# Attention with a cumulative softmax: the half-column products of a unit together, the half-row products together, and the loop over pairs of heads written out

## The chip, the cores and the metric

One core of one Trainium2 chip. The metric is the device time of one execution in microseconds (us). All work lies on five engines: TensorE (PE in the rows; PEld is its loading of the stationary operand), VectorE (DVE), ScalarE (ACT), GpSimd (POOL) and SyncE (SP), which starts the transfers.

## The reference, cut to what matters

```python
x = x + 0.5 * ffn(layernorm(x))        # two experts, top 1
x = x + attn(layernorm(x))             # 16 heads, DK = M = 64, DV = 128, 2 x 1024 tokens
x = x + 0.5 * ffn(layernorm(x))
# attn, for each head, with s clipped to +-32
z = cumlogsumexp(s); g = exp(z_before - z); p = exp(s - z)
hk = hk * g + k (x) p;   ok = q . hk           # step by step over the tokens
pv = softmax(ok)
hv = hv * g + p (x) v;   ov = pv . hv
o = rmsnorm(ov) * silu(gate) @ Wo
```

## The kernel before, in words

The two feed-forward phases are not touched. The attention (`phase_attention`) runs over 8 pairs of heads and, in each pair, over 4 units of 512 tokens (`UNIT`, 4 chunks of 128): 32 units. The first unit of each sequence (`first`) starts from an empty state. The pairs 0 to 6 are the body of a hardware loop on every engine (`Fori`), the last pair is written out, because it also normalises and routes the rows for the last phase.

Inside a unit k of a pair i the recurrence is done in chunks: with e = exp(s) and its running sum z, `ok` is masked scores times e plus the query times the state `hk`, all divided by z; `pv` is its softmax; `ov` is masked scores of pv and e times v, plus pv times the state `hv`. All products that TensorE makes for it stand in the program of one unit in a fixed order, and beside them the projections of the next unit (`project_q`, `project_k`, `project_s`, four `project_vg`: each 12 products of 128x512, in the lines `turned` L1197 and L1223) as filling while other engines work. The order on TensorE before:

1. `project_q(k+1)`; the chunk states `dk` = kn . en (L1284); the scores q . k (L1291); `project_k(k+1)`
2. masked scores times e (L1301); query times `hk` (L1305); `project_s(k+1)`; `okT` turned (L1311); `project_vg` 0; `pv` turned (L1319); `project_vg` 1
3. scores of pv and e, "b" (L1327); the chunk states `dv` = en . v (L1334); masked b times v (L1342); pv times `hv` (L1347); `project_vg` 2 and 3
4. the normed output `u` turned (L1364); e and k of the next unit turned (`turn_ek`, L1260 and L1264); the output projection of this unit, 24 products (L1377)

Two heads are worked on together, 64 rows of the array each. So there are three kinds of product: those over the whole array; those in half columns (the output is 64 partitions high: dk, masked scores times e, dv), written 128\*64 in the rows of the profile; and those in half rows (64 values are summed: scores, b, pv times `hv`), written 64\*128. A product of float32 operands stands in the trace as two; so a run of 8 in the program is x16 there. The projections use fp32r operands split in a high and a low part and stand there once.

VectorE does in a unit: the reciprocal of z (L1072), the running sums of `hk` (L1081, L1083), the mask on the scores (L1088), the copy of k (`k_copy`, L987), `okT` (L1096), the softmax (L1101 to L1109), the mask on b (L1120), the running sums of `hv` (L1128, L1130), gates (L1007), the sum z of the next unit (`z_scan`, L999), the sum of squares (L1152), `u` (L1159), the low part of u turned (L1170), the copy of k turned (`kn_copy`, L1012), and the additions of the output to `xres` (L1177). Its order is that of the program, and every operation waits on semaphores. Two banks of PSUM (`PJ`) take the projections in turn, so `project_q(k+1)` waits for the third gate of unit k, which frees the bank:

```python
def project_q(i, k):
    pe.wait_ge(gate_done, count(i, k, UC, -1))
    turned(i, k, 0, q_mm)
```

## Time and profile before

| | us |
|---|---|
| median of 3 runs | 2142.3 (2140.78 to 2146.86) |
| the profiled execution | 2142.46 |
| its span, first to last instruction | 2140.7 |
| TensorE busy in the span | 2012.2 (94%) |
| VectorE busy in the span | 1371.8 (64%) |
| ScalarE busy in the span | 666.3 (31%) |

The attention takes the span from about 467 to 1717 us. A busy share in the profile is the time in which an instruction of the engine is under way. TensorE's products overlap, so their starts tell more than their durations.

### The profile page before, as it was taken

The page shows a single profiled execution, that of the slowest core. Times are in us where ns is not written, and L with a number is a line of the kernel's source. Part 1 is how long each engine was busy: PE and PEld are TensorE (multiplying, and loading weights), DVE is VectorE, ACT ScalarE, POOL GpSimd, SP SyncE. Part 2 cuts the span into 40 slices and gives each one's busy share as a digit, 9 for nine tenths or more (in the row PEclk, how much of TensorE's full clock was granted, in tenths as well). Part 3 has the DMA queues.
Part 4 walks back from the last instruction along what each step waited for, and adds up shares of the span by engine and source line. Part 5 has one row for each costly group of instructions (what it writes and reads, how often), then busy time and mean ns, then how long its engine had stood idle before and what let it go on. Part 6 is the DMA issues. An engine that isn't in the chain of part 4 may idle for free. (4 is left out here: it accounts for less than half of the span.)

```text
span 2140.7 us, 30741 instructions
## 1 busy us (share of the span) xinstructions
PE 2012.2 (94%) x11848; PEld 1639.8 (77%) x11848; DVE 1371.8 (64%) x2702; ACT 666.3 (31%) x1207; POOL 276.2 (13%) x216
## 2 busy tenths in 40 slices
PE   2999999969999999999999999999999679999998
PEld 2788888847887878878878878878887558888786
DVE  5765667736666666666656666666667756665684
ACT  2443445523121121221212221221213134443452
POOL 2110111101020020120110110110201200110100
PEclk9999999989999999999999999999999789999999
DMA  6463436650010010000000100100100136433565
GB/s 216 142 184 128 134 115 190 202 173 8 1 38 9 1 38 9 17 29 1 28 19 1 38 9 1 38 9 1 38 1 20 40 134 211 128 103 115 149 191 182
DMA packets 54329, 165.14 MB, mean 77 GB/s; under 512 B 5424, under 2 KB 5424, under 8 KB 54192
## 3 DMA queue, kind: packets, MB, share of 16 engines
q1 hardware_dynamic: 46736, 145.80, 21.0%
q0 software_dynamic: 7456, 17.34, 3.9%
q8 instruction: 107, 1.75, 0.3%
q14 instruction: 30, 0.25, 0.0%
HBM read 137.40 MB, written 25.72 MB: 76 GB/s over the span
## 5 line engine op out<-in xcount | busy, mean ns | idle before, releaser
L1223 PE MATMUL at_pj<-at_w_lo,at_xT_hi 128*128 128x512 f32 x512 | 211.2, 413 | 0.0
L1223 PE MATMUL at_pj<-at_w_hi,at_xT_lo 128*128 128x512 f32 x512 | 202.5, 395 | 0.0
L1223 PE MATMUL at_pj<-at_w_hi,at_xT_hi 128*128 128x512 f32 x512 | 202.3, 395 | 0.0
L1197 PE MATMUL at_pj<-at_xT_hi,at_w_lo 128*128 128x512 f32 x384 | 159.2, 414 | 11.9 <-issue 11.1
L550 DVE TENSOR_TENSOR last_ff_w_lo<-last_ff_stage,last_ff_w_hi 128x1024 fp32r<-128x1024 f32 x80 | 98.0, 1225 | 89.3 <-ACT last_ff_w_hi L373 89.1
L1197 PE MATMUL at_pj<-at_xT_hi,at_w_hi 128*128 128x512 f32 x384 | 152.3, 397 | 0.0
L1197 PE MATMUL at_pj<-at_xT_lo,at_w_hi 128*128 128x512 f32 x384 | 151.9, 395 | 0.0
L550 DVE TENSOR_TENSOR first_ff_w_lo<-first_ff_stage,first_ff_w_hi 128x1024 fp32r<-128x1024 f32 x80 | 97.9, 1224 | 77.1 <-ACT first_ff_w_hi L373 76.9
L841 POOL TENSOR_TENSOR at_coef<-at_ms,minus_half 128x4 f32<-128x4 f32 x64 | 63.5, 1008 | 562.6 <-DVE at_ms L1155 562.6
L1177 DVE TENSOR_TENSOR xres<-at_r,xres 128x512 f32<-128x512 f32 x128 | 88.2, 689 | 66.7 <-PE at_r L1377 66.7
L826 POOL TENSOR_TENSOR at_w_lo<-at_stage,at_w_hi 128x1024 fp32r<-128x1024 f32 (+1 forms) x36 | 78.5, 2181 | 400.4 <-ACT at_w_hi L881 400.4
L935 ACT ACTIVATE at_pv<-at_ok 128x512 f32<-128x512 f32 x32 | 20.3, 634 | 333.6 <-DVE at_ok L1103 333.6
L373 ACT ACTIVATE last_ff_w_hi<-last_ff_stage 128x1024 fp32r<-128x1024 f32 x80 | 84.7, 1059 | 126.1 <-PE last_ff_ps_y L666 102.7
L373 ACT ACTIVATE first_ff_w_hi<-first_ff_stage 128x1024 fp32r<-128x1024 f32 x80 | 84.7, 1058 | 115.7 <-PE first_ff_ps_y L666 98.9
L652 PE MATMUL first_ff_ps_h<-first_ff_xT_hi,first_ff_w_lo 128*128 128x512 f32 (+1 forms) x320 | 113.0, 353 | 5.3 <-DVE first_ff_w_lo L550 3.3
L652 PE MATMUL last_ff_ps_h<-last_ff_xT_hi,last_ff_w_lo 128*128 128x512 f32 (+1 forms) x320 | 112.6, 352 | 4.5 <-DVE last_ff_w_lo L550 2.3
L1223 PEld LDWEIGHTS at_pj<-at_w_hi,at_xT_hi 128*128 128x128 f32 x512 | 96.3, 188 | 23.1
L1223 PEld LDWEIGHTS at_pj<-at_w_lo,at_xT_hi 128*128 128x128 f32 x512 | 96.4, 188 | 22.5
L652 PE MATMUL first_ff_ps_h<-first_ff_xT_lo,first_ff_w_hi 128*128 128x512 f32 (+1 forms) x320 | 112.1, 350 | 0.0
L652 PE MATMUL last_ff_ps_h<-last_ff_xT_lo,last_ff_w_hi 128*128 128x512 f32 (+1 forms) x320 | 111.9, 350 | 0.0
L652 PE MATMUL first_ff_ps_h<-first_ff_xT_hi,first_ff_w_hi 128*128 128x512 f32 (+1 forms) x320 | 111.9, 350 | 0.0
L652 PE MATMUL last_ff_ps_h<-last_ff_xT_hi,last_ff_w_hi 128*128 128x512 f32 (+1 forms) x320 | 111.7, 349 | 0.0
(315 smaller groups left out, 4785.6 us busy)
## 6 DMA issues: line engine op xcount, KB each, us to landing
first_ff_stage<-wff SPq DMA_DIRECT2D x90, 512.0 KB, 4.3
last_ff_stage<-wff SPq DMA_DIRECT2D x90, 512.0 KB, 4.2
at_stage<-watt SPq DMA_DIRECT2D x24, 512.0 KB, 3.5
at_stage<-watt SPq DMA_DIRECT2D x16, 384.0 KB, 3.2
xres<-x SPq DMA_DIRECT2D x4, 1024.0 KB, 9.9
mid_rows<-xres SPq DMA_DIRECT2D x4, 1024.0 KB, 7.6
out<-xres SPq DMA_DIRECT2D x4, 1024.0 KB, 7.8
first_ff_xg<-sorted_rows SPq DMA_DIRECT2D x3, 1028.0 KB, 5.3
```

Of the source, the lines that this page charges most:

```text
L373: act.activation(w_hi[:, t % RING, :], stage[:, t % RING, :], ACT.Copy).then_inc(w_hi_done, 1)
L550: dve.tensor_tensor(w_lo[:, t % RING, :], stage[:, t % RING, :], w_hi[:, t % RING, :].bitcast(F32), ALU.subtract).then_inc(w_lo_done, 1)
L652: last = pe.matmul(ps_h[t % 2][:, 0:width], w[:, r, k * P:(k + 1) * P], x[:, k, 0:width], start=(k == 0 and n == 0), stop=(k == KC - 1 and ...
L826: pool.tensor_tensor(w_lo[:, col:col + width], stage[:, 0:width], w_hi[:, col:col + width].bitcast(F32), ALU.subtract).then_inc(piece_lo, 1)
L841: pool.tensor_tensor(coef[:, cols], ms[:, cols], c["minus_half"][:, cols], ALU.pow).then_inc(coef_done, 1)
L935: act.activation(pv[:, :, :], ok[:, :, :], ACT.Exp).then_inc(pv_done, 1)
L1177: dve.tensor_tensor(xres[:, k * UC + cc, :], R[4 + cc % 2][:, :], xres[:, k * UC + cc, :], ALU.add).then_inc(added, 1)
L1197: last = pe.matmul(PJ[(7 * k + part) % 2][:, :], wq(w, kk, part), x[:, kk, tok], start=(kk == 0 and n == 0), stop=(kk == KC - 1 and n == 2))
L1223: last = pe.matmul(PJ[(7 * k + 3 + t) % 2][:, :], x[:, kk, tok], wvg(w, kk), start=(kk == 0 and n == 0), stop=(kk == KC - 1 and n == 2))
```

## The change

On TensorE the products of one kind stand together: dk, masked scores times e and dv (half columns) in one run; b, pv times `hv` and the scores of the next unit (half rows) in another. For that the scores of unit k+1 are made in unit k, with their mask, into a tile `am` that no longer serves b (b has `bm`); and the output projection of unit k moves into unit k+1, between `project_q` and `project_k`. The banks `R` are given out anew. VectorE makes the additions of a unit's output in the next unit, behind the reciprocal, copies k before the sums of `hk`, and makes the sums of `hv` ahead of the softmax. `okT` and `pv` give up their tiles. On all five engines the loop over pairs is written out. In the last pair the statistics of the rows are taken directly behind each addition.

```diff
+bm = sb("at_bm", [P, 2, UC, P])
...
 hv = sb("at_hv", [P, UC, DV])
-okT = sb("at_okT", [P, UNIT])
 ok = sb("at_ok", [P, UC, P])
-pv = sb("at_pv", [P, UC, P])
...
-        sp.dma_start(stage[:, 0:width], watt[bass.ds(pair, 1), :, col:col + width].rearrange("a p n -> (a p) n")).then_inc(piece_loaded, 16)
-    with sp.Fori(0, PAIRS - 1) as i:
+        sp.dma_start(stage[:, 0:width], watt[pair, :, col:col + width]).then_inc(piece_loaded, 16)
+    for i in range(PAIRS - 1):
...
-    with pool.Fori(0, PAIRS - 1) as i:
-        pair(i, False)
-    pair(PAIRS - 1, True)
+    for i in range(PAIRS):
+        pair(i, i == PAIRS - 1)
...
+        for cc in range(UC):
+            dve.wait_ge(wo_mm, count(i, k, UC, cc + 1))
+            dve.tensor_tensor(xres[:, k * UC + cc, :], R[2 + cc % 2][:, :], xres[:, k * UC + cc, :], ALU.add).then_inc(added, 1)
+            if with_statistics:
+                tile_statistics(i, k, cc)
+    def mask_a(i, k):
+        for b in range(2):
+            dve.wait_ge(a_mm, count(i, k, 2, b))
+            dve.tensor_tensor(am[:, b, :, :], R[2 + b][:, :].rearrange("p (a t) -> p a t", a=4),
+                              c["causal"][:, :].rearrange("p (a t) -> p a t", a=1).to_broadcast([P, 4, P]), ALU.mult).then_inc(a_masked, 1)
+    mask_a(0, 0)
     def pair(i, last_pair):
         for k in range(UNITS):
             more = not last_pair or k < UNITS - 1
             first = k % HALVES == 0
             dve.wait_ge(z_done, count(i, k, 1, 1))
             dve.reciprocal(rzT[:, :], zT[:, :]).then_inc(rz_done, 1)
+            if (i, k) != (0, 0):
+                add_out(*((i, k - 1) if k else (i - 1, UNITS - 1)), last_pair and k > 0)
+            if more:
+                k_copy(i, k + 1)
...
-            for b in range(2):
-                dve.wait_ge(a_mm, count(i, k, 2, b))
-                dve.tensor_tensor(am[:, b, :, :],
-                                  R[3 + b][:, :].rearrange("p (a t) -> p a t", a=4),
-                                  c["causal"][:, :].rearrange("p (a t) -> p a t", a=1).to_broadcast([P, 4, P]), ALU.mult).then_inc(a_masked, 1)
-            if more:
-                k_copy(i, k + 1)

             dve.wait_ge(ok_mm, count(i, k, 1, 0))
             dve.wait_ge(rz_done, count(i, k, 1, 1))
-            dve.tensor_tensor(okT[:, :], R[2][:, :], rzT[:, :], ALU.mult).then_inc(ok_scaled, 1)
...
-            dve.wait_ge(ok_tr, count(i, k, 1, 0))
...
-            if last_pair and k > 0:
-                for cc in range(UC):
-                    tile_statistics(i, k - 1, cc)
-                unit_statistics(k - 1)
-            for b in range(2):
-                dve.wait_ge(b_mm, count(i, k, 2, b))
...
+            dve.tensor_tensor(pT[:, :], R[2][:, :], rzT[:, :], ALU.mult).then_inc(ok_scaled, 1)
+
             dve.wait_ge(dv_mm, count(i, k, 1, 0))
             for cc in range(UC if first else UC - 1):
                 to = (cc + 1) % UC
...
+            dve.wait_ge(ok_tr, count(i, k, 1, 0))
...
+            if last_pair and k > 0:
+                unit_statistics(k - 1)
+            for b in range(2):
+                dve.wait_ge(b_mm, count(i, k, 2, b))
+                dve.tensor_tensor(bm[:, b, :, :],
...
+            if more:
+                mask_a(i, k + 1)
             if more:
                 gate_make(i, k + 1, 1)
                 z_scan(i, k + 1)
...
-            for cc in range(UC):
-                dve.wait_ge(wo_mm, count(i, k, UC, cc + 1))
-                dve.tensor_tensor(xres[:, k * UC + cc, :], R[4 + cc % 2][:, :], xres[:, k * UC + cc, :], ALU.add).then_inc(added, 1)
-                if not more:
-                    tile_statistics(i, k, cc)
             if not more:
+                add_out(i, k, True)
                 unit_statistics(k)
-    with dve.Fori(0, PAIRS - 1) as i:
-        pair(i, False)
-    pair(PAIRS - 1, True)
+    for i in range(PAIRS):
+        pair(i, i == PAIRS - 1)
...
+    def scores(i, k):
+        pe.wait_ge(q_out, count(i, k, 1, 1))
+        pe.wait_ge(k_out, count(i, k, 1, 1))
+        for cc in range(UC):
+            for h in range(2):
+                last = pe.matmul(R[2 + h][:, chunk(cc)], kT[half(h), chunk(cc)], qT[half(h), k % 2, chunk(cc)], start=True, stop=True)
+                if cc == UC - 1:
+                    last.then_inc(a_mm, 1)
+    def project_out(i, k, next_masked):
+        if k == 0:
+            pe.wait_ge(piece_lo, i * NP + 1 + 5)
+        if next_masked:
+            pe.wait_ge(a_masked, count(i, k + 1, 2, 2))
+        if i == PAIRS - 1 and k > 0:
+            pe.wait_ge(rows_ready, k)
+        for cc in range(UC):
+            if cc % 2 == 0:
+                pe.wait_ge(u_lo, count(i, k, 2, cc // 2 + 1))
+            if cc >= 2:
+                pe.wait_ge(added, count(i, k, UC, cc - 1))
+            for h in range(2):
+                for n, (x, w) in enumerate(((uT_lo, w_hi), (uT_hi, w_lo), (uT_hi, w_hi))):
+                    last = pe.matmul(R[2 + cc % 2][:, :], x[:, cc // 2, h, (cc % 2) * P:(cc % 2 + 1) * P], wo(w, h),
+                                     start=(h == 0 and n == 0), stop=(h == 1 and n == 2))
+            last.then_inc(wo_mm, 1)
     turn_ek(0, 0)
+    scores(0, 0)
...
             if more:
                 project_q(i, k + 1)
+            if (i, k) != (0, 0):
+                project_out(*((i, k - 1) if k else (i - 1, UNITS - 1)), True)
+            if more:
+                project_k(i, k + 1)

             pe.wait_ge(en_out, count(i, k, 1, 1))
             pe.wait_ge(kn_out, count(i, k, 1, 1))
-            pe.wait_ge(added, count(i, k, UC, 0))
             for cc in range(UC if first else UC - 1):
...
-            pe.wait_ge(q_out, count(i, k, 1, 1))
-            for cc in range(UC):
-                for h in range(2):
-                    last = pe.matmul(R[3 + h][:, chunk(cc)], kT[half(h), chunk(cc)], qT[half(h), b2, chunk(cc)], start=True, stop=True)
-                    if cc == UC - 1:
-                        last.then_inc(a_mm, 1)
-            if more:
-                project_k(i, k + 1)
-
-            pe.wait_ge(u_lo, count(i, k, 2, 0))
+            pe.wait_ge(added, count(i, k, UC, 0))
             pe.wait_ge(a_masked, count(i, k, 2, 2))
             for cc in range(UC):
                 for h in range(2):
                     last = pe.matmul(R[2][half(h), chunk(cc)], en[:, cc, half(h)], am[:, h, cc, :],
                                      start=(cc == 0), stop=(first and cc == 0), skip_group_check=True)
+            pe.wait_ge(v_out, count(i, k, UC, UC))
+            for cc in range(UC if first else UC - 1):
+                for h in range(2):
+                    last = pe.matmul(R[5][half(h), chunk(cc)], en[:, cc, half(h)], v[:, b2, cc, h * DV:(h + 1) * DV],
+                                     start=True, stop=True)
+            last.then_inc(dv_mm, 1)
             pe.wait_ge(hk_done, i * HK_AT[UNITS] + HK_AT[k + 1] + 1)
...
             pe.wait_ge(p_out, count(i, k, 1, 1))
+            pe.wait_ge(hv_done, i * HK_AT[UNITS] + HK_AT[k + 1] + 1)
             for cc in range(UC):
                 for h in range(2):
                     last = pe.matmul(R[4 + h][:, chunk(cc)], eT[half(h), b2, chunk(cc)], pT[half(h), chunk(cc)], start=True, stop=True)
                     if cc == UC - 1:
                         last.then_inc(b_mm, 1)
-            pe.wait_ge(v_out, count(i, k, UC, UC))
-            for cc in range(UC if first else UC - 1):
+            for cc in range(1 if first else 0, UC):
                 for h in range(2):
-                    last = pe.matmul(R[2][half(h), chunk(cc)], en[:, cc, half(h)], v[:, b2, cc, h * DV:(h + 1) * DV],
-                                     start=True, stop=True)
-            last.then_inc(dv_mm, 1)
+                    pe.matmul(R[h][:, chunk(cc)], pT[half(h), chunk(cc)], hv[half(h), cc, :],
+                              start=(cc == (1 if first else 0)), stop=False, skip_group_check=True)
+            if more:
+                scores(i, k + 1)
             for h in range(2):
                 pe.wait_ge(b_masked, count(i, k, 2, h + 1))
                 for cc in range(UC):
-                    last = pe.matmul(R[h][:, chunk(cc)], am[:, h, cc, :], v[:, b2, cc, h * DV:(h + 1) * DV],
-                                     start=(cc == 0), stop=(first and cc == 0), skip_group_check=True)
-            pe.wait_ge(hv_done, i * HK_AT[UNITS] + HK_AT[k + 1] + 1)
-            for cc in range(1 if first else 0, UC):
-                for h in range(2):
-                    last = pe.matmul(R[h][:, chunk(cc)], pT[half(h), chunk(cc)], hv[half(h), cc, :],
+                    last = pe.matmul(R[h][:, chunk(cc)], bm[:, h, cc, :], v[:, b2, cc, h * DV:(h + 1) * DV],
                                      start=False, stop=True, skip_group_check=True)
-                    if cc == UC - 1:
-                        last.then_inc(o_mm, 1)
+                last.then_inc(o_mm, 1)
             if more:
                 project_vg(i, k + 1, 2)
                 project_vg(i, k + 1, 3)
             if last_pair and k > 0:
                 pe.wait_ge(is1_done, k)
+                if more:
+                    pe.wait_ge(a_masked, count(i, k + 1, 2, 2))
                 pe.matmul(rt_later, c["later"][:], routing["is1"][:, tiles(k - 1)], start=True, stop=True).then_inc(rank_mm, 1)
                 pe.matmul(rt_total, c["ones"][:], routing["is1"][:, tiles(k - 1)], start=True, stop=True).then_inc(rank_mm, 1)
...
             if more:
                 turn_ek(i, k + 1)
-            if k == 0:
-                pe.wait_ge(piece_lo, i * NP + 1 + 5)
-            for cc in range(UC):
-                if cc % 2 == 0:
-                    pe.wait_ge(u_lo, count(i, k, 2, cc // 2 + 1))
-                if cc >= 2:
-                    pe.wait_ge(added, count(i, k, UC, cc - 1))
-                for h in range(2):
-                    for n, (x, w) in enumerate(((uT_lo, w_hi), (uT_hi, w_lo), (uT_hi, w_hi))):
-                        last = pe.matmul(R[4 + cc % 2][:, :], x[:, cc // 2, h, (cc % 2) * P:(cc % 2 + 1) * P], wo(w, h),
-                                         start=(h == 0 and n == 0), stop=(h == 1 and n == 2))
-                last.then_inc(wo_mm, 1)
-    with pe.Fori(0, PAIRS - 1) as i:
-        pair(i, False)
-    pair(PAIRS - 1, True)
```

In the order of the program on TensorE, the second unit, from the last product of a projection to the first of the next one, before (names: output <- moving, stationary operand; `x7` is seven more of the row):

```order
L1197 MATMUL at_pj<-at_xT_hi,at_w_hi 128x512
L1284 MATMUL at_r<-at_en,at_kn 64x64 [waits at_added,at_kn_out,at_en_out]
L1284 MATMUL at_r<-at_en,at_kn 64x64 x5
L1291 MATMUL at_r<-at_qT,at_kT 128x128 [waits at_q_out]
L1291 MATMUL at_r<-at_qT,at_kT 128x128 x7
L1206 REGISTER_ALU
L1197 MATMUL at_pj<-at_xT_hi,at_w_lo 128x512 [waits at_gate_done]
```

and with the change:

```order
L1201 MATMUL at_pj<-at_xT_hi,at_w_hi 128x512
L1319 MATMUL at_r<-at_en,at_kn 64x64 [waits at_kn_out,at_en_out]
L1319 MATMUL at_r<-at_en,at_kn 64x64 x5
L1326 MATMUL at_r<-at_am,at_en 64x128 [waits at_a_masked,at_added]
L1326 MATMUL at_r<-at_am,at_en 64x128 x7
L1331 MATMUL at_r<-at_v,at_en 64x128 [waits at_v_out]
L1331 MATMUL at_r<-at_v,at_en 64x128 x5
L1336 MATMUL at_r<-at_qT,at_hk 128x128 [waits at_hk_done]
L1336 MATMUL at_r<-at_qT,at_hk 128x128 x3
L1201 MATMUL at_pj<-at_xT_hi,at_w_lo 128x512 [waits at_q_out]
```

What moved: the scores have left, `project_k` no longer parts dk from the masked scores times e, and dv has come in from the later place.

Still TensorE, behind `project_vg` 1 in the same unit, before:

```order
L1223 MATMUL at_pj<-at_w_hi,at_xT_hi 128x512
L1327 MATMUL at_r<-at_pT,at_eT 128x128 [waits at_p_out]
L1327 MATMUL at_r<-at_pT,at_eT 128x128 x7
L1334 MATMUL at_r<-at_v,at_en 64x128 [waits at_v_out]
L1334 MATMUL at_r<-at_v,at_en 64x128 x5
L1340 REGISTER_ALU
L1342 MATMUL at_r<-at_v,at_am 128x128 [waits at_b_masked]
L1342 MATMUL at_r<-at_v,at_am 128x128 x3
L1342 MATMUL at_r<-at_v,at_am 128x128 [waits at_b_masked]
L1342 MATMUL at_r<-at_v,at_am 128x128 x3
L1347 MATMUL at_r<-at_hv,at_pT 128x128 [waits at_hv_done]
L1347 MATMUL at_r<-at_hv,at_pT 128x128 x7
```

and with the change:

```order
L1227 MATMUL at_pj<-at_w_hi,at_xT_hi 128x512
L1359 MATMUL at_r<-at_pT,at_eT 128x128 [waits at_hv_done,at_p_out]
L1359 MATMUL at_r<-at_pT,at_eT 128x128 x7
L1364 MATMUL at_r<-at_hv,at_pT 128x128 x8
L1276 MATMUL at_r<-at_qT,at_kT 128x128 [waits at_k_out,at_q_out]
L1276 MATMUL at_r<-at_qT,at_kT 128x128 x7
L1371 MATMUL at_r<-at_v,at_bm 128x128 [waits at_b_masked]
L1371 MATMUL at_r<-at_v,at_bm 128x128 x3
L1371 MATMUL at_r<-at_v,at_bm 128x128 [waits at_b_masked]
L1371 MATMUL at_r<-at_v,at_bm 128x128 x3
```

What moved: dv has left, pv times `hv` stands directly behind b, and the scores of the next unit follow.

Still TensorE, at the end of the same unit, from u to the first product of what follows, before:

```order
L1364 MATMUL at_r<-ident,at_u 128x128 [waits at_u_done]
L1364 MATMUL at_r<-ident,at_u 128x128 x3
L1364 MATMUL at_r<-ident,at_u 128x128 [waits at_u_done]
L1364 MATMUL at_r<-ident,at_u 128x128 x3
L1260 MATMUL at_r<-ident,at_eT 128x128 [waits at_e_done]
L1260 MATMUL at_r<-ident,at_eT 128x128 x3
L1264 MATMUL at_r<-ident,at_kT 128x128 [waits at_k_out]
L1264 MATMUL at_r<-ident,at_kT 128x128 x3
L1377 MATMUL at_r<-at_w_hi,at_uT_lo 128x512 [waits at_u_lo]
```

and with the change, where the projection of q follows directly:

```order
L1389 MATMUL at_r<-ident,at_u 128x128 [waits at_u_done]
L1389 MATMUL at_r<-ident,at_u 128x128 x3
L1389 MATMUL at_r<-ident,at_u 128x128 [waits at_u_done]
L1389 MATMUL at_r<-ident,at_u 128x128 x3
L1264 MATMUL at_r<-ident,at_eT 128x128 [waits at_e_done]
L1264 MATMUL at_r<-ident,at_eT 128x128 x3
L1268 MATMUL at_r<-ident,at_kT 128x128 [waits at_k_out]
L1268 MATMUL at_r<-ident,at_kT 128x128 x3
L1201 MATMUL at_pj<-at_xT_hi,at_w_lo 128x512 [waits at_gate_done]
```

What moved: the first product behind the turned k waits for a gate, where it waited for the low part of u.

## Rows read from the trace of the kernel before

**Rows 1.** The page of the profile: busy time, share of the span, instructions

```profile
PE 2012.2 (94%) x11848; PEld 1639.8 (77%) x11848; DVE 1371.8 (64%) x2702; ACT 666.3 (31%) x1207; POOL 276.2 (13%) x216
```

**Rows 2.** Stretches of the attention: us, busy per engine, then granted clock

```profile
650.00:800.00 150.00, 148.99 (x978) 121.13 (x979) 94.78 (x191) 32.62 (x69) 20.69 (x14) 0.99 0.06 17
1250.00:1400.00 150.00, 147.70 (x973) 119.78 (x972) 95.04 (x191) 32.61 (x69) 20.66 (x14) 0.99 0.06 17
1555.00:1595.00 40.00, 39.81 (x266) 32.22 (x267) 27.28 (x51) 8.12 (x18) 4.39 (x3) 1.00 0.00 1
```

**Rows 3.** TensorE in time order, first half of a unit: start, busy, group

```profile
842.23 0.39 PE L1197 MATMUL at_pj<-at_xT_hi,at_w_hi 128*128 128x512 f32 x1
842.55 0.57 PE L1284 MATMUL at_r<-at_en,at_kn 128*64 128x64 f32 x12
843.05 1.16 PE L1291 MATMUL at_r<-at_qT,at_kT 64*128 64x128 f32 x16
844.14 0.50 PE L1197 MATMUL at_pj<-at_xT_hi,at_w_lo 128*128 128x512 f32 x1
844.48 0.40 PE L1197 MATMUL at_pj<-at_xT_lo,at_w_hi 128*128 128x512 f32 x1
...
858.44 1.16 PE L1327 MATMUL at_r<-at_pT,at_eT 64*128 64x128 f32 x16
```

**Rows 4.** The same view, the end of the unit before

```profile
821.24 1.16 PE L1327 MATMUL at_r<-at_pT,at_eT 64*128 64x128 f32 x16
...
825.34 0.94 PE L1347 MATMUL at_r<-at_hv,at_pT 64*128 64x128 f32 x12
826.21 0.50 PE L1223 MATMUL at_pj<-at_w_lo,at_xT_hi 128*128 128x512 f32 x1
...
831.91 1.04 PE L1364 MATMUL at_r<-ident,at_u 128*128 128x128 f32 x8
...
834.01 0.47 PE L1377 MATMUL at_r<-at_w_hi,at_uT_lo 128*128 128x512 f32 x1 [0.19 <-DVE at_uT_lo L1170]
```

**Rows 5.** TensorE in time order, just behind an edge of the loop

```profile
650.51 0.50 PE L1197 MATMUL at_pj<-at_xT_hi,at_w_lo 128*128 128x512 f32 x1 [2.12 <-issue]
...
655.04 0.69 PE L1284 MATMUL at_r<-at_en,at_kn 128*64 128x64 f32 x16
655.66 1.16 PE L1291 MATMUL at_r<-at_qT,at_kT 64*128 64x128 f32 x16
```

**Rows 6.** The waits: engine and line, releaser, total us, times, longest

```profile
PEld at_pj L1197 <- issue: 13.7, 6, 2.6
```

**Rows 7.** VectorE in time order, the same unit

```profile
822.44 1.29 DVE L1120 TENSOR_TENSOR at_am<-at_r,causal 128x512 f32<-128x512 f32 x2 [2.78 <-PE at_r L1327]
...
825.02 0.42 DVE L1007 SCALAR_TENSOR_TENSOR at_gate<-at_gate,at_pj 128x256 f32<-128x256 f32 x1
...
827.01 0.69 DVE L1152 TENSOR_REDUCE at_ss<-at_u 128x4 f32<-128x512 f32 x1 [0.37 <-ACT at_u L954]
...
829.99 2.16 DVE L1159 SCALAR_TENSOR_TENSOR at_u<-at_r,at_coef,at_gate 128x128 f32<-128x128 f32 x8 [1.29 <-POOL at_coef L841]
833.17 0.69 DVE L1170 TENSOR_TENSOR at_uT_lo<-at_r,at_uT_hi 128x512 fp32r<-128x512 f32 x1 [1.02 <-ACT at_uT_hi L963]
833.78 0.41 DVE L1007 SCALAR_TENSOR_TENSOR at_gate<-at_gate,at_pj 128x256 f32<-128x256 f32 x1
...
835.75 0.68 DVE L1177 TENSOR_TENSOR xres<-at_r,xres 128x512 f32<-128x512 f32 x1
...
843.73 1.38 DVE L1083 TENSOR_TENSOR at_hk<-at_r,at_hk 64x64 f32<-64x64 f32 x6
...
847.21 0.69 DVE L987 COPY at_kT<-at_pj 128x512 f32<-128x512 f32 x1 [0.78 <-PE at_pj L1197]
```

**Rows 8.** VectorE, then TensorE, in the last unit of all

```profile
1674.71 3.34 DVE L1072 RECIPROCAL at_rzT<-at_zT 128x512 f32<-128x512 f32 x1
...
1680.82 1.98 PE L1301 MATMUL at_r<-at_am,at_en 128*64 128x128 f32 x16 [4.22 <-DVE at_am L1088]
```

57 lines of the change are left out of this document (30 added, 27 removed).

## The prediction

> **What bounds the kernel now.** I read the page first: TensorE is busy for 94% of the span [rows 1], so a change that leaves it its work can only give back what lies between the products. The windows of the attention show it busy nearly without a break, 149.0 and 147.7 of 150 us, at 0.99 of the full clock [rows 2]. So I went on to the starts of the products in time order, where a busy share shows nothing: a product counts as under way while the array is being switched. From one b to the next a unit takes 858.44 - 821.24 = 37.20 us [rows 3, 4].
>
> **What a switch between kinds costs.** The starts of a projection are 0.233 us apart (24 of them and a late second one fill the 5.70 from 826.21 to 831.91 [rows 4]). Around the half-array runs they are not.
> - Before a half run the first start is late: 842.55 - 842.23 = 0.32, 0.09 over the pitch [rows 3].
> - A run of 12 half-row products lasts 826.21 - 825.34 = 0.87 [rows 4], one of 16 lasts 844.14 - 843.05 = 1.09 [rows 3]. Four more cost 0.22, 0.055 each, so 0.20 of each run is no product.
> - Half columns of 64 wide: 12 last 0.50 [rows 3], 16 last 655.66 - 655.04 = 0.62 [rows 5]. That is 0.03 each and about 0.14 fixed.
> - Behind a half run the second start of the full array is late too: 844.48 - 844.14 = 0.34, 0.10 over [rows 3].
>
> A unit has now three runs of half columns (fixed 0.14), three of half rows (0.20), and on the side of the full array four entries to a half run (0.09) and four returns (0.10): 0.42 + 0.60 + 0.36 + 0.40 = 1.78 us. With the change there is one run of each kind, two entries and two returns: 0.14 + 0.20 + 0.18 + 0.20 = 0.72. **1.06 us less a unit**, if a start on a new tile and bank inside a run costs nothing, which no row here can show for certain.
>
> The rows thus give 0.14 to 0.20 for a switch. The Trainium skill, "TensorEngine Tiling (Array Packing)", section "Key Properties", says that a change of the tiling mode drains the TensorE, and agrees in kind, without a price. From "TensorE: Matmul & The Clock Gate", sections "Step-by-step: what each phase is for" and "LDWEIGHTS", a drain of 128 cycles (53 ns) and an uncovered load of 128 columns (107 ns) would make an estimate of 0.16, so 0.96 for the six switches removed; the rows have the word.
>
> **New waits on TensorE.** I walked one unit of the new order with the durations above.
> - *hk.* The query times `hk` product needs the running sums, which start once dk is out. Now the scores and `project_k` (4 us) lie between. Then only masked scores times e and dv do. Count from dk's first product, 12-product kind: the run of 12 + 16 + 12 lasts 0.36 + 28 x 0.055 + 0.14 = 2.04. VectorE copies k first. `project_k`'s last product starts at 844.48 + 10 x 0.233 = 846.81 [rows 3], a half run would follow 0.32 later, at 847.13, and the copy starts at 847.21 [rows 7]; so it starts 0.1 behind dk, and holds VectorE for 0.6; six updates take 1.38 [rows 7], the signal about 0.12 (the 834.01 start behind the 833.86 end of the low part is 0.15 [rows 4, 7]). 0.1 + 0.6 + 1.38 + 0.12 = 2.2: a wait of 0.2. In the other kind eight updates (1.84) stand against 0.48 + 32 x 0.055 + 0.14 = 2.38: 2.67, a wait of 0.3. **+0.25 a unit**, bounds 0 and 0.5. The scores' mask no longer stands on this path.
> - *u.* TensorE comes to u 0.54 earlier: of the four switches between b and u now (0.14 + 0.20 + 0.19 + 0.20) one of 0.20 is left, and the scores take dv's place. VectorE now starts the mask on b 1.20 behind b, its next gate 3.78 behind, and could start the sum of squares 0.37 before 827.01, so at 5.40; it starts at 5.77 [rows 4, 7]. With the change the mask of the scores waits for a run of 44 (0.20 + 43 x 0.055, and the 0.3 by which the mask follows now): 2.75; two masks 1.29, then gate and z 1.62: 5.66. Not later. u then starts 2.98 on (829.99 - 827.01), its first half is out at 9.9, and TensorE arrives at 10.67 - 0.54 = 10.13. Covered, by 0.2; in the other kind (hv has 16) by less than 0.1. It costs nothing while that holds.
> - *gate.* Behind the turned k now comes `project_q`, which waits for the third gate. In the trace that gate ends at 834.19 [rows 7]; with the same 0.15 the start would be at 834.34, where the output projection started at 834.01 [rows 4] (itself 0.4 late for the low part of u). The chain up to it (u turned, ScalarE's copy, the low part, the gate) is unchanged and starts with u turned. **+0.33 a unit**, bounds 0 and 0.5.
> - *added.* The third tile of the output projection waits for the first addition, which now stands behind the reciprocal. From the start of the gate (833.78) VectorE is free 1.97 later (835.75 [rows 7]), the reciprocal takes 3.34 [rows 8], the addition and signal 0.8: 6.1. TensorE: 0.56 to `project_q`, 2.9 for it, twelve products 2.8: 6.25. Just covered; a late VectorE would cost TensorE here one for one.
>
> The transfers of weights and their split lie one unit of 37 us deep in slack, and no engine gets more work (a mask is moved, none added). Sum per unit: -1.06 + 0.25 + 0.33 = **-0.48**.
>
> **The loop.** At each edge TensorE waits for nothing that the profile shows, 2.12 us at the first [rows 5]; there are six, 13.7 us for the loads together [rows 6]. The start is 2.1 late: 6 x 2.1 = 12.6. The two stretches with a granted clock of 0.99 [rows 2] hold an edge each; 0.01 of 150 us is 1.5, and I take this as the clock's answer to the idle time: 3.0 more. **-15.6**. The last pair is straight code already; its first unit runs 266 products in 40 us, 6.6 a us, at full clock, as many as the loop (978 in 150) [rows 2]. So I charge nothing for longer code.
>
> **The last pair.** In units 1 and 2 of it VectorE's routing holds TensorE; I take 0. In the last unit the reciprocal starts at 1674.71, behind the additions, and masked scores times e waited 4.22 until 1680.82 [rows 8]. With the change the reciprocal is done before the additions, and the mask is there; then the sums of `hk` end some 3.5 earlier, and 2.5 us of statistics leave the middle of the chain to the softmax and routing. I take **-5**, bounds 0 and -8.
>
> **Sum.** 29 units (28 of the loop, the first of the last pair) x -0.48 = -13.9; -15.6; -5. Together -34.5 on the profiled execution's 2142.46, which is the median (2142.3) but for 0.2: **2108 us**.
>
> **The rivals.**
> - *No new wait* (0.15): VectorE's sums come in time and the gate's order does no harm. Then 29 x 0.58 = 17 more is saved: 2091. For it: each of the two is a difference of 0.2 to 0.3 in a walk. Against it: the gate's end is read straight from a row.
> - *Long half runs slow down* (0.08). A run of 44 or 48 products is three times as long as any now, and if their issue, not the array, sets the pace once what was queued is used up, both runs grow by 0.3: 29 x 0.6 = 17 us worse, 2125. Against it: b and dv stand together now, 32 products, and the 16 half rows keep 0.055 to the end [rows 3]. The Trainium skill, "TensorE: Matmul & The Clock Gate", section "Wait — 56ns, not 53.3ns?", gives about 62 ns for a MATMUL decoded in software; 48 x 7 ns would be 0.3.
> - *The cost is not the kind's* (0.05) but that of any group of small products which begins behind a wait; then joining them leaves it, 1.06 returns in 29 units: 2108 + 31 = 2139, no change that can be told. Against it: dk to scores pays 0.2 although both are small.
> - *Slower* (0.05): the addition behind the reciprocal. It is covered by 0.1 us. Each us by which VectorE comes later to the copy of k keeps TensorE's third tile waiting a us in each unit; from 34.5 / 29 = 1.2 us it decides. With 1.5 the time is 2108 + 29 x 1.5 = 2151. For it: VectorE takes the mask of the scores, the gate and z in a row before u. Against it: the walk finds these in time.
>
> **How the numbers follow.** My own forecast has 0.57, and with its bounds (hk 0 to 0.5, gate 0 to 0.5, last unit 0 to -8) reaches from 2093 to 2122; mixed cases of it with more waiting have the remaining 0.10, about 2126. The range takes in the rival without waits and the one of long runs: 2084 to 2128; outside lie the last two and the tails. Two executions of this kernel differ by about 0.3%, so faster means under 2136, and takes all but the last two rivals: 0.90; same 0.05; slower 0.05.
>
> **What would show it.** TensorE in time order: one run of x40 or x48 half columns lasting 2.0 to 2.4, and one of x44 or x48 half rows; query times `hk` with an idle time of 0.2 to 0.3 released by VectorE's `at_hk`; the first product of `project_q` idle for 0.4 to 0.7, released by `at_gate`; no idle for issue at four-unit distances; units of 36.6 to 36.8. A wait of the output projection for `xres`, or u later than TensorE, would make the time longer; products closer together behind the switches shorter.

## The result

| | before | after |
|---|---|---|
| median, us | 2144.2 (2140.8 to 2146.9, 4 runs) | 2108.8 (2105.6 to 2111.2, 4 runs) |
| profiled execution, us (span) | 2142.5 (2140.7) | 2111.2 (2109.5) |
| ratio, 95% interval | | 0.9835 (0.9812 to 0.9857) |

The change saves 35 us by these medians. In the experiments below the kernel before has medians of 2141.6 to 2142.2 (9 runs each); beside those it is 33. TensorE keeps its share of 94%, but of a shorter span; its products are as many as before [rows 1]. The page of the profile after:

```profile
PE 1982.6 (94%) x11848; PEld 1629.8 (77%) x11848; DVE 1365.2 (65%) x2702; ACT 669.6 (32%) x1207; POOL 278.8 (13%) x216
```

The two stretches of [rows 2], asked of the kernel after, hold 997 and 998 products instead of 978 and 973, at a granted clock of 1.00 in both. The columns are those of [rows 2].

```profile
650.00:800.00 150.00, 148.13 (x997) 122.31 (x996) 97.41 (x195) 33.54 (x70) 20.62 (x14) 1.00 0.06 17
1250.00:1400.00 150.00, 148.12 (x998) 122.27 (x998) 97.81 (x197) 34.85 (x73) 20.63 (x14) 1.00 0.06 17
```

TensorE in time order, kernel after, one unit (it answers to [rows 3, 4]). Look at the starts: the run dk, masked scores times e, dv begins at 875.36; b, hv and scores at 888.20; then masked b times v.

```profile
875.03 0.40 PE L1201 MATMUL at_pj<-at_xT_hi,at_w_hi 128*128 128x512 f32 x1
875.36 0.69 PE L1319 MATMUL at_r<-at_en,at_kn 128*64 128x64 f32 x16
875.87 1.04 PE L1326 MATMUL at_r<-at_am,at_en 128*64 128x128 f32 x16
876.75 1.04 PE L1331 MATMUL at_r<-at_v,at_en 128*64 128x128 f32 x16
878.08 0.94 PE L1336 MATMUL at_r<-at_qT,at_hk 128*128 128x128 f32 x6 [0.29 <-DVE at_hk L1098]
878.77 0.48 PE L1201 MATMUL at_pj<-at_xT_hi,at_w_lo 128*128 128x512 f32 x1
...
887.87 0.40 PE L1227 MATMUL at_pj<-at_w_hi,at_xT_hi 128*128 128x512 f32 x1
888.20 1.16 PE L1359 MATMUL at_r<-at_pT,at_eT 64*128 64x128 f32 x16
889.19 0.84 PE L1364 MATMUL at_r<-at_hv,at_pT 64*128 64x128 f32 x12
889.86 1.06 PE L1276 MATMUL at_r<-at_qT,at_kT 64*128 64x128 f32 x16
890.85 2.05 PE L1371 MATMUL at_r<-at_v,at_bm 128*128 128x128 f32 x16
892.66 0.48 PE L1227 MATMUL at_pj<-at_w_lo,at_xT_hi 128*128 128x512 f32 x1
```

Entry to a half run: 875.36 - 875.03 = 0.33. Inside the run of half columns the next kind of product comes without a loss: 16 of dk last 0.51, 0.032 each, and nothing is added before 875.87. Inside the run of half rows 16 of b last 0.99 and 12 of hv 0.67: a start costs 0.06 on average, also on a new tile. Behind it, 890.85 - 889.86 = 0.99 holds 16 scores and one switch.

The `hk` product above waits for VectorE, and `project_q` for the third gate. The same view, the end of this unit; and the waits of the weight loads (engine and line, releaser, total us, times, longest), which begin ahead of the products' own and so are longer than what TensorE loses:

```profile
898.34 1.18 PE L1389 MATMUL at_r<-ident,at_u 128*128 128x128 f32 x8
899.35 0.60 PE L1264 MATMUL at_r<-ident,at_eT 128*128 128x128 f32 x4
899.79 0.60 PE L1268 MATMUL at_r<-ident,at_kT 128*128 128x128 f32 x4
900.77 0.47 PE L1201 MATMUL at_pj<-at_xT_hi,at_w_lo 128*128 128x512 f32 x1 [0.38 <-DVE at_gate L1004]
...
906.15 0.40 PE L1294 MATMUL at_r<-at_w_hi,at_uT_hi 128*128 128x512 f32 x1
906.39 0.39 PE L1294 MATMUL at_r<-at_w_hi,at_uT_lo 128*128 128x512 f32 x1
```

```profile
PEld at_r L1389 <- DVE at_u L1168: 17.4, 35, 4.2
...
PEld at_r L1336 <- DVE at_hk L1098: 14.2, 32, 0.6
...
PEld at_pj L1201 <- DVE at_gate L1004: 9.4, 22, 0.5
```

One more wait is there that the prediction had at nothing, for `at_u`: the eight transposes of u last 899.35 - 898.34 = 1.01 in this unit. The third tile of the output projection (906.39) follows at the pitch, 0.24 behind the start ahead of it. VectorE in time order, kernel after, shows what these products wait for (it answers to [rows 7]):

```profile
875.46 0.69 DVE L984 COPY at_kT<-at_pj 128x512 f32<-128x512 f32 x1 [2.06 <-PE at_pj L1201]
876.09 0.46 DVE L1096 COPY at_hk<-at_r 64x64 f32<-64x64 f32 x2
...
896.64 2.16 DVE L1168 SCALAR_TENSOR_TENSOR at_u<-at_r,at_coef,at_gate 128x128 f32<-128x128 f32 x8 [1.31 <-POOL at_coef L840]
899.60 0.69 DVE L1179 TENSOR_TENSOR at_uT_lo<-at_r,at_uT_hi 128x512 fp32r<-128x512 f32 x1 [0.80 <-ACT at_uT_hi L961]
900.21 0.41 DVE L1004 SCALAR_TENSOR_TENSOR at_gate<-at_gate,at_pj 128x256 f32<-128x256 f32 x1
...
902.18 3.34 DVE L1083 RECIPROCAL at_rzT<-at_zT 128x512 f32<-128x512 f32 x1
905.44 0.63 DVE L1067 TENSOR_TENSOR xres<-at_r,xres 128x512 f32<-128x512 f32 x1
```

The first addition ends at 905.44 + 0.63 = 906.07, just ahead of that tile.

To read all units and not one, I took from the starts in the trace, for each group of products, the mean time from its first start to the first start of the next group, over the 28 units from the first dk to that of the last pair (for the kernel before the median where a loop's edge falls in). The other columns are kernels of the experiments below.

| us | before | after | gate ahead | k behind | hv apart | VectorE late | kn behind |
|---|---|---|---|---|---|---|---|
| dv's last start to `hk` product | (0.20) | 0.47 | 0.47 | 0.42 | 0.47 | 0.48 | 0.42 |
| u, 8 transposes | 0.87 | 1.09 | 1.09 | 1.09 | 0.87 | 1.09 | 1.09 |
| turned k, 4 transposes, and the wait behind them (before for u's low part, then for the gate) | 0.70 | 0.83 | 0.36 | 0.84 | 1.05 | 0.84 | 0.36 |
| output projection | 5.68 | 5.58 | 6.02 | 5.58 | 5.58 | 7.13 | 5.58 |
| whole unit | 37.12 | 36.61 | 36.55 | 36.56 | 37.00 | 38.17 | 36.06 |

(The unit of before is that of the kernel with the loop written out, which has no edges. 0.20 is a switch without a wait.)

By stretches of the profiled executions, us:

| | before | after | difference |
|---|---|---|---|
| start to the first dk | 502.6 | 509.3 | +6.7 |
| 28 units, dk to dk | 1055.1 | 1025.1 | -30.0 |
| last pair, its first dk to the last feed-forward's first product | 170.5 | 161.3 | -9.2 |
| from there to the end of the span | 412.6 | 413.8 | +1.2 |

4.0 us of the first line are only order: 16 scores and 12 products of `project_k` now stand between the first turned e and the first dk (7.8 us instead of 3.7), and are missing in the last pair. Without them the start is 2.7 longer (6.70 - 4.04) and the last pair 5.1 shorter (9.17 - 4.04). The last pair varies by itself: its second unit lasts 39.4 and 41.0 us in the two executions of one kernel (experiment 1), so that differences of 1 us there say little.

### The profile page after: what moved, and what is told of

It reads as the page before. It is cut to its first block and busy times, and to the rows that moved or that the text cites. A ratio compares the mean times of both kernels' runs of the same rounds, so it can differ in the third digit from the quotient of the medians.

```text
span 2109.5 us, 29738 instructions
## 1 busy us (share of the span) xinstructions
PE 1982.6 (94%) x11848; PEld 1629.8 (77%) x11848; DVE 1365.2 (65%) x2702; ACT 669.6 (32%) x1207; POOL 278.8 (13%) x216
## 5 line engine op out<-in xcount | busy, mean ns | idle before, releaser
L933 ACT ACTIVATE at_ok<-at_ok 128x512 f32<-128x512 f32 x32 | 20.3, 633 | 412.2 <-DVE at_ok L1122 412.2
L1227 PEld LDWEIGHTS at_pj<-at_w_hi,at_xT_lo 128*128 128x128 f32 x512 | 96.5, 188 | 19.0
```

The lines of the kernel that those rows point to most:

```text
L933: act.activation(ok[:, :, :], ok[:, :, :], ACT.Exp).then_inc(pv_done, 1)
L1227: last = pe.matmul(PJ[(7 * k + 3 + t) % 2][:, :], x[:, kk, tok], wvg(w, kk), start=(kk == 0 and n == 0), stop=(kk == KC - 1 and n == 2))
```

## The experiments

The ratios are to the kernel before, measured on the same chip with the kernel; "28 units" is the stretch of the table above.

**1. The loop alone.** The kernel before, with the loop written out on each of the five engines (TensorE's shown):

```diff
-            with pe.Fori(0, PAIRS - 1) as i:
-                pair(i, False)
-            pair(PAIRS - 1, True)
+            for i in range(PAIRS):
+                pair(i, i == PAIRS - 1)
```

> The kernel before with nothing changed but the loop over pairs, written out on all five engines. My theory: the loop's part of the change is worth 15.6 us (six edges of 2.1 us each and 3.0 us of clock), so about 16 us under the kernel before: 2127 to 2129. The units keep their 37.2 us. Rival: the longer straight code costs TensorE something (code has to be fetched), and the edges' 12.6 us come back only in part: 2132 or more, with starts of products further apart than 0.233 us somewhere. Other rival: the clock owes nothing to the edges, then 12.6 alone, about 2131.

Measured: 2131.9 us beside 2141.7, ratio 0.9949 (0.9934 to 0.9964), 9.8 less. The 28 units last 1039.3 instead of 1055.1: 15.8 less, as forecast. Units keep their 37.0 to 37.2 and starts their 0.23. So the code of eight pairs in place of two costs TensorE nothing in the loop, and what is missing of the 15.8 lies outside it: the first dk comes at 505.8, not 502.6.

The edges are not all alike. In the trace of the kernel before, a unit over an edge of the loop lasts 39.1 to 39.5 us at four of the six, 1.9 to 2.3 more than the 37.2 of the same unit written out, at a granted clock of 1.00. At the first and the fifth it lasts 41.2 and 40.6, and behind these two the granted clock is 0.50 for 3.4 us (651.5 to 654.9, and 1255.6 to 1259.0). The first of them:

```profile
651.50:654.50 3.00, 3.00 (x8) 2.31 (x8) 0.88 (x1) 0.00 (x0) 0.00 (x0) 0.50 0.00 0
```

Windows of the start of the attention show where the later first dk comes from; this one first of the kernel with the loop written out, then of the kernel before:

```profile
472.00:475.00 3.00, 3.00 (x8) 2.32 (x8) 3.00 (x6) 0.00 (x0) 0.00 (x0) 0.50 0.03 12
```

```profile
472.00:475.00 3.00, 3.00 (x15) 2.45 (x14) 3.00 (x7) 0.61 (x2) 0.00 (x0) 1.00 0.05 19
```

TensorE starts 8 products where it started 15, at half the clock, and again at 493 to 496.5 (0.54, beside 1.00). I ran both kernels again.

> The same kernel as in the run with the loop over pairs alone written out, once more. There the loop's stretch of the trace was 15.8 us shorter, but the time only 9.8; in its trace the first dk came 3.2 us later than in the kernel before, with a stretch of half clock at the start of the attention that the kernel before did not have. Theory: that stretch comes by chance, from one execution to the next, and the median over more runs is 12 to 14 us under the kernel before. Rival: the written-out code brings it each time, and the median stays 10 under.

> The kernel before once more, for a second trace of its start. Theory (chance): the time from the first product of the attention's first projection to the turned e, 27.3 us in its trace, may be anywhere from 27.3 to 31, as in the traces of the written-out kernels. Rival (the loop's code): again 27.3.

Measured: 2131.3 beside 2142.2, ratio 0.9944 (0.9930 to 0.9957). The 28 units 1039.4 against 1054.8. The first dk at 506.0 (505.8 in the first trace), and in the kernel before at 502.9 (502.6). So my theory of chance falls for these two kernels: each repeats its own start in both its traces. But "written-out code brings it" does not hold either: from the attention's first projection to the turned e the kernels of experiments 2 and 8 below, also written out, need 27.3 us like the kernel before in both its traces; the others need 28.6 to 30.9, this one 31.0 twice, the kernel after 29.4.

The time goes with the clock. Where the stretch lasts 27.3 us (before, experiments 2 and 8) the granted clock is 1.00 in all of it. The kernel after (29.4) has 0.50 from its start at 472.1 to 476.7; the kernel of experiment 4 (28.7) has 1.00 at 472 and 0.50 from 491.5 to 494.9; this one (31.0) has both. What decides which stretches are at half clock stays open. It costs up to 3.7 us. The rest of what is missing lies in the last pair, 0.5 and 1.4 us longer than before in the two traces, and in the last feed-forward, +1.0 and -1.3.

**2. The gate's wait.** The kernel after, the third gate ahead of both low parts of u on VectorE:

```diff
-                        if more and b == 1:
+                        if more and b == 0:
                             gate_make(i, k + 1, 2)
```

> The changed kernel with the third gate made ahead of both low parts of u on VectorE, not between them. My theory: project_q waits for that gate, 0.25 to 0.35 us a unit, and this wait goes: 28 to 31 units x 0.3 = 8 to 9 us less than the changed kernel, about 2100. The first low part of u is 0.6 us later, under 2.9 us of project_q. Rival: the wait only moves, to ScalarE's tanh or to the second half of u, and the time stays at 2109.

Measured: 2106.6, ratio 0.9832 (0.9817 to 0.9847), which can't be told from the kernel after. The wait is gone entirely: turned k to `project_q` 0.36 instead of 0.83. And the output projection lasts 6.02 instead of 5.58. TensorE in time order, and VectorE, in this kernel:

```profile
901.77 0.47 PE L1294 MATMUL at_r<-at_w_hi,at_uT_lo 128*128 128x512 f32 x1 [0.28 <-DVE xres L1067]
...
894.27 0.41 DVE L1004 SCALAR_TENSOR_TENSOR at_gate<-at_gate,at_pj 128x256 f32<-128x256 f32 x1
895.16 0.69 DVE L1179 TENSOR_TENSOR at_uT_lo<-at_r,at_uT_hi 128x512 fp32r<-128x512 f32 x1 [0.48 <-ACT at_uT_hi L961]
...
897.73 3.34 DVE L1083 RECIPROCAL at_rzT<-at_zT 128x512 f32<-128x512 f32 x1
900.99 1.23 DVE L1067 TENSOR_TENSOR xres<-at_r,xres 128x512 f32<-128x512 f32 x2
```

Its third tile starts at 901.77, behind the first addition (900.99), which stands behind the reciprocal. Of the 0.48 saved 0.43 come back there: the addition had 0.05 us of cover in the kernel after. It is neither of my two rivals but the one the prediction had called just covered.

**3. The wait for hk.** The kernel after, with the copy of k behind the sums:

```diff
-                    if more:
-                        k_copy(i, k + 1)
                     dve.wait_ge(dk_mm, count(i, k, 1, 0))
                     ...
                         dve.wait_ge(hk_done, i * HK_AT[UNITS] + HK_AT[k] + cc + 2)
+                    if more:
+                        k_copy(i, k + 1)
```

> The changed kernel with the copy of k behind the running sums of hk on VectorE, not ahead of them. My theory: the wait of the query times hk product (0.27 us a unit in the trace) is VectorE's 0.6 us for this copy, so it goes entirely: 32 x 0.27 = 8.6 us less, about 2100. Rival: the sums are late by themselves (dk's end and 1.4 to 1.8 us of updates), and the wait stays at 0.1 or more: 2105. Nothing else should move, since the next reader of k is the next unit's first project_vg, 3 us on.

Measured: 2107.1, ratio 0.9834 (0.9820 to 0.9848). In time this can't be told from the kernel after. In the starts the gap falls from 0.47 to 0.42 only; the rival holds. VectorE in this kernel, behind a dk that starts at 875.95:

```profile
876.68 0.46 DVE L1094 COPY at_hk<-at_r 64x64 f32<-64x64 f32 x2 [2.69 <-PE at_r L1319]
877.17 1.44 DVE L1096 TENSOR_TENSOR at_hk<-at_r,at_hk 64x64 f32<-64x64 f32 x6
878.65 0.69 DVE L984 COPY at_kT<-at_pj 128x512 f32<-128x512 f32 x1
```

The first sum starts 0.73 behind dk; with the copy ahead of it, in the kernel after, it is 876.09 - 875.36 = 0.73 too. The copy fills the time in which dk ends and its signal arrives. In units with 12 products of dk the copy does count a little: there the gap falls from 0.38 to 0.29, with 16 it stays at 0.56. What TensorE waits for is in the main the chain of updates itself.

**4. Both.** Edits 2 and 3 together.

> The changed kernel with both orders of VectorE changed: third gate ahead of the low parts of u, copy of k behind the sums of hk. My theory: the two waits are independent, and both savings add up: 17 us under the changed kernel, about 2092; a unit lasts 36.05 us. Rival: one wait takes over what the other loses (u is then the only thing near TensorE), and the sum is under 12 us: 2097 or more.

Measured: 2105.9, ratio 0.9823 (0.9807 to 0.9840), again not to be told from the kernel after, and a unit of 36.50: the rival, since the third tile has taken over the gate's wait.

**5. The fourth gate and kn behind the second addition.** Edits 2 and 3, and the two operations between u's low part and the reciprocal moved:

```diff
-            def add_out(i, k, with_statistics):
+            def add_out(i, k, with_statistics, behind=lambda: None):
                 ...
+                    if cc == 1:
+                        behind()
...
-                        add_out(*(...), last_pair and k > 0)
+                        add_out(*(...), last_pair and k > 0, lambda: (gate_make(i, k, 3), kn_copy(i, k)))
...
-                    if more:
-                        gate_make(i, k + 1, 3)
-                        kn_copy(i, k + 1)
```

> The kernel with both orders of VectorE changed (third gate ahead of the low parts of u, copy of k behind the sums of hk), and in addition the fourth gate and the copy of the turned k (kn) behind the second addition, not ahead of the reciprocal. The trace of the kernel with both has TensorE's third tile of the output projection 0.44 us late in each unit, released by the first addition, which stands behind these two (0.9 us) and the reciprocal. My theory: they come 0.9 us earlier, and the wait goes: 28 x 0.44 = 12 us less than that kernel, 2093 to 2094, a unit of 36.06 us. Rival: project_k waits for the fourth gate or dk for kn in its place (both are now made while TensorE computes tiles 3 and 4, 2.8 us): no gain, 2106.

Measured: 2092.5 us, ratio 0.9765 (0.9752 to 0.9778), a unit of 36.06. It is the fastest kernel of the study, 0.7% under the kernel after. VectorE there: the reciprocal starts sooner behind u, and gate and kn lie between two additions, where it waited for TensorE.

```profile
895.65 3.34 DVE L1085 RECIPROCAL at_rzT<-at_zT 128x512 f32<-128x512 f32 x1
898.98 0.69 DVE L1067 TENSOR_TENSOR xres<-at_r,xres 128x512 f32<-128x512 f32 x1
...
900.98 0.41 DVE L1004 SCALAR_TENSOR_TENSOR at_gate<-at_gate,at_pj 128x256 f32<-128x256 f32 x1
901.31 0.68 DVE L1009 COPY at_kn<-at_r 128x512 f32<-128x512 f32 x1
901.91 0.68 DVE L1067 TENSOR_TENSOR xres<-at_r,xres 128x512 f32<-128x512 f32 x1
```

**6. One run of half columns more.** Edit 3, and `project_k` between dk and masked scores times e:

```diff
-                    if more:
-                        project_k(i, k + 1)
                     pe.wait_ge(en_out, count(i, k, 1, 1))
                     ...
                     last.then_inc(dk_mm, 1)
+                    if more:
+                        project_k(i, k + 1)
```

> The changed kernel with the copy of k behind the sums of hk, and with project_k between dk and masked scores times e, so that the half columns make two runs in place of one. Against the kernel with the copy of k behind alone. My theory: one run more of half columns costs its fixed 0.14 us, an entry of 0.09 and a return of 0.10: 0.33 x 31 units = 10 us more, so about 2110 where the other has 2100. Rival (a switch costs nothing, only a group behind a wait does): no difference between the two, since nothing waits there in either.

Measured: 2111.3, ratio 0.9854 (0.9836 to 0.9871), beside 0.9834 of experiment 3, where the intervals overlap; by the starts a unit lasts 36.69, 0.13 longer. This looks like too little, because the wait for hk, which experiment 3 had not removed, goes here (the sums have `project_k` to themselves): 0.22 of it. TensorE in this kernel:

```profile
874.21 0.69 PE L1317 MATMUL at_r<-at_en,at_kn 128*64 128x64 f32 x16
...
877.78 1.09 PE L1326 MATMUL at_r<-at_am,at_en 128*64 128x128 f32 x16
878.71 1.04 PE L1331 MATMUL at_r<-at_v,at_en 128*64 128x128 f32 x16
879.68 0.94 PE L1336 MATMUL at_r<-at_qT,at_hk 128*128 128x128 f32 x6
```

The gap ahead of the `hk` product is now 0.20, a switch alone. With the wait put back, the run more costs 0.13 + 0.22 = 0.35, beside 0.33 from the rows of before.

**7. One run of half rows more.** The kernel after, with the product of hv behind masked b times v again:

```diff
-                    for cc in range(1 if first else 0, UC):
-                        for h in range(2):
-                            pe.matmul(R[h][:, chunk(cc)], pT[...], hv[...], ...)
                     if more:
                         scores(i, k + 1)
                     ... (masked b times v)
+                    for cc in range(1 if first else 0, UC):
+                        for h in range(2):
+                            last = pe.matmul(R[h][:, chunk(cc)], pT[...], hv[...], ...)
```

> The changed kernel with the product of hv back behind masked b times v, where it stood before, so that the half rows make two runs in place of one. My theory: one run more of half rows costs 0.20 us fixed and 0.19 for entry and return: 0.39 x 32 = 12 us more, about 2121; up to 7 us above that if the squares of the output, which are then released later, push u behind TensorE. Rival: no cost of kinds, 2109.

Measured: 2122.3, ratio 0.9915 (0.9902 to 0.9929); a unit lasts 37.00, 0.39 longer, the forecast price. From b to the end of the gates' projections TensorE needs 10.65 instead of 10.25, so all of it lies in the switches. u has no stall any more (0.87), and the wait for the gate is longer by the same 0.22: the two are one chain, which TensorE meets at one place or the other.

**8. VectorE 1.6 us late.** The kernel after, with one reciprocal more whose result is not used:

```diff
+                    dve.reciprocal(bm[:, 0, 0:2, :]..., zT[:, 0:UNIT // 2])
                     dve.reciprocal(rzT[:, :], zT[:, :]).then_inc(rz_done, 1)
```

> The changed kernel with a second, half as wide reciprocal (its result is not used) ahead of the one of each unit: VectorE comes 1.7 us later to the first addition. The rival of the prediction says that each us beyond the cover keeps TensorE's third tile waiting a us. The addition is out 0.3 us before TensorE comes in the changed kernel, so 1.4 us a unit, 1.7 in the last pair: 28 x 1.4 + 3 x 1.7 = 44 us more, about 2153. If other work of VectorE caught the delay up, or TensorE had more cover than the 0.3 us seen, the time would stay under 2130.

Measured: 2155.8, ratio 1.0061 (1.0045 to 1.0076): slower than the kernel before. VectorE and TensorE:

```profile
916.16 1.74 DVE L1083 RECIPROCAL at_bm<-at_zT 128x256 f32<-128x256 f32 x1
917.83 3.29 DVE L1084 RECIPROCAL at_rzT<-at_zT 128x512 f32<-128x512 f32 x1
921.04 1.22 DVE L1067 TENSOR_TENSOR xres<-at_r,xres 128x512 f32<-128x512 f32 x2
...
921.81 0.47 PE L1295 MATMUL at_r<-at_w_hi,at_uT_lo 128*128 128x512 f32 x1 [1.27 <-DVE xres L1067]
```

The addition starts 921.04 - 916.16 = 4.88 behind the first reciprocal's start, instead of 905.44 - 902.18 = 3.26: 1.62 later. A unit is 1.55 longer. The rest, 0.07, was cover; the expectation had 0.3, since it left out the 0.16 from the end of an addition to the start that waits for it (901.77 - 900.99 - 0.62 in experiment 2), and read one unit alone.

**9. The last unit's reciprocal.** The kernel after, where in the last unit alone the reciprocal stands behind the additions:

```diff
-                    dve.wait_ge(z_done, count(i, k, 1, 1))
-                    dve.reciprocal(rzT[:, :], zT[:, :]).then_inc(rz_done, 1)
+                    (the same two, under: if more)
                     ... (the additions)
+                    if not more:
+                        dve.wait_ge(z_done, count(i, k, 1, 1))
+                        dve.reciprocal(rzT[:, :], zT[:, :]).then_inc(rz_done, 1)
```

> The changed kernel with the reciprocal of the very last unit behind the additions, where it stood before; all else as changed. In that unit the sums of hk then end 3.3 us later, and the third tile of the output projection is free of its 1.3 us behind the reciprocal: TensorE comes to query times hk 2 us later after the start of the unit before, and this is the whole of the reciprocal's part in the last unit's gain. If it were all of that gain it would be 8 us later.

One execution, 2113.1 us; the trace is what counts here. TensorE's `hk` product of the last unit, in the kernel after and in this one:

```profile
1652.89 1.16 PE L1336 MATMUL at_r<-at_qT,at_hk 128*128 128x128 f32 x8 [0.32 <-DVE at_hk L1098]
```

```profile
1653.22 2.08 PE L1340 MATMUL at_r<-at_qT,at_hk 128*128 128x128 f32 x8 [3.53 <-DVE at_hk L1102]
```

From the dk of the unit before it comes 1.6 us later (41.6 against 40.0), near the 2 expected. But from that dk to the last feed-forward's first product it is 3.6 us (86.4 against 82.8): behind the longer wait TensorE goes on at half clock (the eight `hk` products are busy for 2.08, above for 1.16). The window behind that wait, in this kernel; in the kernel after the clock from 1652 to 1656 is 1.00:

```profile
1653.20:1656.00 2.80, 2.08 (x8) 1.78 (x8) 0.61 (x1) 0.00 (x0) 0.00 (x0) 0.50 0.00 0
```

In the kernel after the granted clock is at 0.50 from 1657.7 for 6.8 us, in this one from 1652.8 for 13.7. I count from the dk named above, because the unit ahead of it, which the edit does not touch, is 0.9 shorter in this execution (41.0 against 41.9). The kernels of experiments 2 to 5, which have the reciprocal ahead too, need 82.8 to 83.3 for the same stretch. So the reciprocal is worth some 3.1 to 3.6 of the last pair's 5.1. What gives the rest, the statistics that moved, the clock or chance, was not tried.

## Why the prediction was right

It forecast 2108 us with 2108.8 measured, and the mechanisms of its main terms held as far as they were tested. Two of the small terms were wrong and cancel each other (u and the gate):

| step | forecast | measured | by |
|---|---|---|---|
| six switches less, a unit | -1.06 | -1.12 | what is left of the unit (-0.506) without the three waits (0.615) |
| a run of half columns / half rows | 0.33 / 0.39 | 0.35 / 0.39 | experiments 6, 7 |
| wait for hk | +0.25 | +0.27 | table, 0.47 - 0.20 |
| u | 0 | +0.22 | table |
| wait for the gate | +0.33 | +0.13 | table, 0.83 - 0.70 |
| addition behind the reciprocal | 0, cover 0.1 | 0, cover 0.05 to 0.07 | experiments 2, 8 |
| unit | -0.48 | -0.51 | 36.61 - 37.12 |
| loop, in its stretch | -15.6 | -15.8, -15.4 | experiment 1, twice |
| last pair but for its first unit | -5 | -4.7 | -5.1 + 0.4 |

- **Switches.** The cost belongs to the change of kind, not to a small group or a new tile. The rival by which "the cost is not the kind's" falls with experiments 6 and 7, in which products that nobody waits for cost 0.35 and 0.39 a unit when they are set apart. The rows gave the fixed part of a run, 0.14 and 0.20; the Trainium skill, "TensorEngine Tiling (Array Packing)", "Key Properties", says that a change of tiling mode drains the TensorE, and the runs agree, with these numbers for the price.
- **Long half runs.** They did not slow down: 16 b and 12 hv and 16 scores keep 0.06 a start to the end, and 44 of them last 890.85 - 888.20 = 2.65, with 0.20 + 44 x 0.055 = 2.62 from the rows of before. The 0.3 us for a longer MATMUL that the prediction took from the Trainium skill, "TensorE: Matmul & The Clock Gate", section "Wait — 56ns, not 53.3ns?", is not seen.
- **hk.** The size was right and the reason partly wrong. The prediction put the copy of k on the path ("it starts 0.1 behind dk, and holds VectorE for 0.6"); experiment 3 shows that the copy lies beside dk's own end, in the kind with 16 of dk entirely and with 12 but for 0.09.
- **u and the gate.** This is the step that erred in its parts: "Covered, by 0.2". (Its printed terms for the mask, 0.20 + 43 x 0.055 + 0.3, make 2.87 and not 2.75; the trace has 890.96 - 888.20 = 2.76, so the walk goes on from the right figure.) Covered is true of u's first half, which the walk looked at. The second half is not ready when TensorE has turned the first (VectorE needs 1.08 for four, TensorE 0.44), and TensorE stands 0.22. As the gate's chain starts with u turned, the prediction's +0.33 behind it contains this time: 0.22 + 0.13 = 0.35. Experiment 7 moves it from the one to the other: without the stall the gate costs 1.05 - 0.70 = 0.35.
- **The slower rival.** Its mechanism is real and was nearer than its chance of 0.05 says: 1.6 us on VectorE make the kernel slower than before (experiment 8), as "from 1.2 us it decides" and "With 1.5 the time is 2151" had it. It decided the fate of the two improvements too, and moving it gave the third.
- **The loop.** Edges cost 15.8 in the stretch where they are, clock included. The 3.0 for the clock was read from the two stretches of [rows 2] alone and is right for all six edges, since those two stretches hold just the two edges with half clock behind them. In the time only 10 to 11 of it arrive (experiment 1), mostly since the start came 3.1 to 3.2 later. That a changed program may meet another clock at its start had no term in the sum; in the kernel after the start is 2.7 us longer, 2.1 of it in this way and 0.6 ahead of the attention's first projection. The 28 units gave 30.0 where 29.0 were forecast. The spans of the two traces differ by less than the 34.5 of the sum: -30.0 - 5.1 + 2.7 + 1.2 = -31.2. The medians are 35 apart, as the profiled execution after is the longest of its four and that of before lies 1.8 under its median. So that 2108 was met to within 1 us is in part luck: the start was left out of the sum, and the spread of the executions (2105.6 to 2111.2 after, 2140.8 to 2146.9 before) made it good.
- **The last pair.** Of the -5 the part that was tested, the reciprocal, is 3.1 to 3.6, as the 3.5 by which the sums of hk were to end earlier. The part of the statistics is argued only, and the spread of 1 us there makes the close agreement of -4.7 chance.
- **The bounds.** The ends given for hk, gate and the last unit, all taken at once, reach from 2088 to 2125 us, not from 2093 to 2122; the range of 2084 to 2128 holds both.

## What to carry to other kernels

Where TensorE is busy all the time, read the starts, not the busy share: a change between whole array, half rows and half columns costs some 0.1 to 0.2 us each way, and products of one kind may stand together across tiles and banks for nothing. When such a regrouping takes the slack out, walk every hand-over in halves, and find the second wait behind the first: here a wait of 0.48 us hid one of 0.43 in another engine's order, and only with both gone did 16 us come. Six edges of 2 us and more were worth writing out: 10 to 11 us of the 15.8 arrived in the time. The longer code cost TensorE nothing in the units themselves; what it has to do with the later start in that kernel stays open.
